# A decoder in one kernel: gated attention's weights and first tiles made in the product keys' last pair

## The reference, cut to what matters

```python
# L0_ffn: product keys
xn = (x - mu) * rsqrt(var + eps) * gamma + beta          # over all tokens
q = (xn @ w_q.T).reshape(b, n, 2, h, kd)                 # h = 8, kd = 128
sim = einsum('pbnhd,hkpd->pbnhk', q, keys)               # 64 keys an axis
s, i = top_k(sim, 8)                                     # then top 8 of the 64 sums
scores, pk = top_k(all_scores, 8); idx = ...             # 64 picks of 4096 rows a token
o = einsum('bnd,bnhkd->bnhk', inputs, key_in[idx])
o = gelu(o) * softmax(scores)
y = einsum('bnhk,bnhkd->bnd', o, key_out[idx])

# L1_attn: gated attention, 16 heads of 16
Q, K, V = (x @ W.T + b for W, b in ((Wq, bq), (Wk, bk), (Wv, bv)))
Qn = Q / max(norm(Q), 1e-12); Kn = K / max(norm(K), 1e-12)      # per head
attn = softmax(Qn @ Kn.T / sqrt(16)); head_outs = attn @ V
h = gelu(x @ Wg1.T + bg1); logits = (h @ Wg2.T + bg2).mean(1)
out = (head_outs * sigmoid(g) * sigmoid(logits)) @ Wo.T + bo
```

## Time and profile before

| | us |
|---|---|
| runs shown | 1965.34, 1972.49, 1965.74; median 1965.74 |
| profiled execution | 1975.05, its span 1973.3 |
| TensorE busy | 1824.4 (92%) |
| VectorE busy | 1331.3 (67%) |
| ScalarE busy | 658.1 (33%) |
| GpSimd busy | 268.0 (14%) |
| mean granted TensorE clock | 0.967 |

### The profile page before, as it was taken

One profiled execution on the slowest core, in us unless ns is written; L12 is line 12 of the kernel. 1 busy time (PEld: TensorE's weight loads), 2 busy tenths in 40 slices (PEclk: granted clock), 3 DMA queues, 4 the chain that ended last, 5 costly groups with the idle time before them and its releaser, 6 DMA issues. The chain is left out here.

```text
span 1973.3 us, 44245 instructions
## 1 busy us (share of the span) xinstructions
PE 1824.4 (92%) x16947; PEld 1539.4 (78%) x16947; DVE 1331.3 (67%) x3614; ACT 658.1 (33%) x1520; POOL 268.0 (14%) x200
## 2 busy tenths in 40 slices
PE   5999999699758999999999959988899999999998
PEld 4888787477557888888888836667788888888887
DVE  4566655377658888989888647746665666666664
ACT  2444443244342212211221126636332323333232
POOL 3222232311010000000000057711000000000000
PEclk9999999799878999999999979989999999999999
DMA  4000000222042000000000040000211111212101
GB/s 161 2 1 0 0 0 1 49 65 64 1 103 38 6 0 5 5 5 0 5 5 0 2 121 1 0 13 27 33 26 23 20 28 16 32 16 32 16 0 43
DMA packets 139266, 47.73 MB, mean 24 GB/s; under 512 B 108178, under 2 KB 138418, under 8 KB 139186
## 3 DMA queue, kind: packets, MB, share of 16 engines
q1 hardware_dynamic: 139186, 46.66, 10.3%
HBM read 42.43 MB, written 4.19 MB: 24 GB/s over the span
## 5 line engine op out<-in xcount | busy, mean ns | idle before, releaser
L2833 ACT ACTIVATE m_silu<-m_gate 128x512 f32<-128x512 f32 x136 | 81.5, 600 | 379.0 <-PE m_gate L621 379.0
L2914 DVE TENSOR_TENSOR m_act_up<-m_silu,m_up 128x512 f32<-128x512 f32 x136 | 93.6, 688 | 168.4 <-PE m_up L621 124.9
L2898 DVE SCALAR_TENSOR_TENSOR g_x<-m_y,m_combine,g_x 128x256 f32<-128x256 f32 x272 | 118.8, 479 | 51.8 <-PE m_y L621 50.3
L237 ACT ACTIVATE a_prob<-a_score,a_neg_max 128x128 f32<-128x128 f32 x256 | 90.7, 367 | 162.5 <-DVE a_neg_max L227 162.5
L2469 PE MATMUL f_out<-f_ko,f_gel 128*128 128x256 f32 x512 | 122.5, 390 | 2.0 <-issue 1.3
L2512 ACT ACTIVATE f_gel<-f_act 128x512 f32<-128x512 f32 x128 | 76.6, 598 | 130.4 <-PE f_act L621 90.9
L2469 PE MATMUL f_turn<-f_ko,f_gel 128*128 128x256 f32 x512 | 111.8, 379 | 0.0
L621 PE MATMUL f_act<-f_hT_pair_high,f_kiT_high 128*128 128x256 f32 x384 | 108.2, 282 | 0.0
L2469 PEld LDWEIGHTS f_out<-f_ko,f_gel 128*128 128x128 f32 x512 | 95.1, 192 | 16.5 <-issue 3.9
L2469 PEld LDWEIGHTS f_turn<-f_ko,f_gel 128*128 128x128 f32 x512 | 97.3, 190 | 13.2
L621 PE MATMUL f_act<-f_hT_pair_high,f_kiT_low 128*128 128x256 f32 x384 | 107.3, 279 | 0.0
(11 more groups left out here) (390 smaller groups left out, 5189.1 us busy)
## 6 DMA issues: line engine op xcount, KB each, us to landing
f_gel<-in_L_ffn_key_in SPq DMA_DIRECT2D x16, 256.0 KB, 4.6
f_ko<-in_L_ffn_key_out SPq DMA_DIRECT2D x2, 2048.0 KB, 19.0
g_shared<-in_ctx SPq DMA_DIRECT2D x8, 256.0 KB, 2.7
fp_wq_nat<-in_L_ffn_w_q SPq DMA_DIRECT2D x8, 256.0 KB, 3.0
h_kept<-fp_hT SPq DMA_DIRECT2D x8, 256.0 KB, 2.6
g_shared<-h_kept SPq DMA_DIRECT2D x8, 256.0 KB, 3.0
g_ctx_next<-in_ctx SPq DMA_DIRECT2D x8, 256.0 KB, 2.7
g_ctx_all<-in_ctx SPq DMA_DIRECT2D x1, 2048.0 KB, 10.6
```

The source lines that it names most:

```text
L237: last = act.activation(self.prob[:, u % 4, j, :], self.score_bank[u % 2][:, j // 2, (j % 2) * P:(j % 2 + 1) * P], ACT.Exp, bias=self.neg_ ...
L2833: act.activation(silu[:, m, :], gate_bank[m][:, :], ACT.Silu).then_inc(silu_ready[m].sem, 1)
L2898: last = dve.scalar_tensor_tensor(x[:, tile, :], y_bank[n][:, t * D:(t + 1) * D], weight, x[:, tile, :], ALU.mult, ALU.add)
L2914: dve.tensor_tensor(act_up[:, m, :], silu[:, m, :], up_bank[m][:, :], ALU.mult) \
```

## The change

Four things.

- The weights, small inputs and first work of gated attention move into the last pair of the product keys, into memory that the low parts (`kiT_low`, `fused_low`) no longer need: SyncE issues the loads when the last activations are done; 7 transpose jobs stand among the outputs of block 0, with all copies on ScalarE; among the outputs of block 1 stand the transposes of pair 0's norm and its two products for queries and keys. VectorE makes the norms of pair 0 and 1 and the statistics of pair 2, empties and sums the squares; GpSimd makes the roots and the two powers of pair 0.
- Gated attention starts with pair 1's norm, and every engine first waits until SyncE has counted up the stage's semaphores (`counts_begun`).
- 28 rows are split in place of 24, so 14 of 16 jobs of the preparation are split ones; the similarities stand behind steps 2 to 5.
- `row_hot` holds three groups in place of four. The last group's rows are made by an instruction of their own behind the first group's weights, into the first group's place. GpSimd's `pair_remainder` waits until the one-hot tiles of the pair before are made.

```diff
 class Turner:
+    def turn(self, pe, n):
+        blocks, _ = self.jobs[n]
+        pe.wait_ge(self.copied[n % 2], n // 2)
+        at = 0
+        for b in blocks:
+            rows = b.shape[0]
+            last = pe.transpose(self.banks[n % 2][:, at:at + rows], b, self.ident[0:rows, 0:rows])
+            at += rows
+        last.then_inc(self.turned[n % 2], 1)
...
+    def all_on_act(self, act):
+        self._copy(act, act.copy, (0, 1))
 # stage_gated_attention
         def _(sp):
-            for n, w in enumerate((w_q, w_k, w_v, w_o)):
-                sp.dma_start(w_nat[:, 2 * n:2 * n + 2, :], w.rearrange("(t p) n -> p t n", p=P)).then_inc(w_loaded, 16)
...
+            sp.sem_inc(counts_begun, 1)
             load_next(sp)
         def _(pool):
-            ln.setup(pool)
-            pool.memset(inv_power[:, :], -0.5).then_inc(power_set, 1)
-            pool.wait_ge(power_set, 1)
-            ln.root(pool, 0)
+            pool.wait_ge(counts_begun, 1)
+            ln.root(pool, 2)
             pool.memset(ones[:, :, :], 0.0).then_inc(masks_cut, 1)
...
-            ln.root(pool, 1)
-            ln.root(pool, 2)
-            for n in range(2):
-                for b in range(2):
-                    invert(n, n, b)
-            pool.wait_ge(loaded, N_LOADS * 16)
+            for b in range(2):
+                given.invert(pool, 1, ss[1], inv[1], b)
         def _(pe):
+            pe.wait_ge(counts_begun, 1)
-            produce(-2, "xn", 0)
-            pe.wait_ge(w_loaded, N_WEIGHTS * 16)
-            turner.on_pe(pe)
-            turner.wait_all(pe)
-            ring.wait_emptied(pe, -2, "xn")
-            produce(-2, "qk0", 0)
-            produce(-2, "qk1", 0)
             produce(-1, "xn", 1)
             produce(-1, "hidden", 0)
         def _(act):
-            empty(-2, "xn", 0, 0)
-            turner.on_act(act)
-            act.wait_ge(loaded, N_LOADS * 16)
-            act.activation(static[:, :], g_row[:, :], ACT.Exp, scale=-1.0).then_inc(static_exp, 1)
-            square(-2, 0, 0, 0)
-            empty(-1, "xn", 1, 1)
-            square(-2, 0, 0, 1)
+            act.wait_ge(given.loaded, given.N_LOADS * 16)
+            empty(-1, "xn", 1, 1)
             act.activation(static[:, :], g_row[:, :], ACT.Exp, scale=-1.0).then_inc(static_exp, 1)
             empty(-1, "hidden", 0, 0)
         def _(dve):
-            ln.statistics(dve, 0)
-            ln.apply(dve, 0)
-            ln.statistics(dve, 1)
-            turner.on_dve(dve)
...
+            dve.tensor_scalar(bg2_neg[:, :], bg2[:, :], -1.0, None, ALU.mult)
+            scale_heads(0, 0, 0)
+            scale_heads(0, 0, 1)
             dve.wait_ge(static_exp, 1)
...
             dve.sem_inc(wide_ready, 1)
-            dve.wait_ge(loaded, N_LOADS * 16)
-            empty(-2, "qk0", 0, 0)
-            ln.apply(dve, 1)
-            empty(-2, "qk1", 0, 0)
-            ln.statistics(dve, 2)
-            sum_squares(0, 0, 0)
-            sum_squares(0, 0, 1)
             empty(-1, "qk0", 1, 1)
             ln.apply(dve, 2)
 # stage_product_keys, preparation
-    SPLIT = 24
+    SPLIT = 28
-                return range(WHOLE + 2 * i, WHOLE + 2 * i + 2) if i < 4 else range(WHOLE + i + 4, WHOLE + i + 5)
+                return range(WHOLE + 2 * i, WHOLE + 2 * i + 2) if i < 6 else range(WHOLE + i + 6, WHOLE + i + 7)
 # stage_product_keys
-        row_hot = s.sb("row_hot", [P, HALF, P], F16)
+        row_hot = s.sb("row_hot", [P, GU - 1, GT, P], F16)
-        TURN_AT, SIMS_AT, SECOND_AT = 0, 3, (23, 24, 26, 28)
+        TURN_AT, SIMS_AT, SECOND_AT = 0, 2, (23, 24, 26, 28)
+        turner = Turner(s, sim_bank, ident, "gated")
+        turner.weight(gated.w_nat, gated.wT, 9)
+        turner.jobs.append(([gated.wg2], gated.wg2T))
+        JOBS_AT = tuple(range(8, 8 + 2 * JOBS, 2))
+        XN_AT, QK_AT = 0, (4, 9)
         def _(sp):
+            sp.wait_ge(act_ready[1], 8 * PAIRS)
+            gated.load(sp)
         def _(pool):
                     pool.wait_ge(h_high, i + 1)
+                    if not (isinstance(i, int) and i == 0):
+                        pool.wait_ge(hot_ready, 2 * i)
...
+            gated.ln.root(pool, 0)
+            gated.ln.root(pool, 1)
+            pool.wait_ge(g_ready[1].sem, g_ready[1].at(NB - 1, 1))
+            pool.memset(gated.inv_power, -0.5).then_inc(gated.power_set, 1)
+            pool.wait_ge(gated.power_set, 1)
+            for b in range(2):
+                gated.invert(pool, 0, gated.ss, gated.inv, b)
         def _(pe):   # weight_group
+                    if m == GU - 1:
+                        pe.wait_ge(last_hot_ready, n + 1)
         # second_weights(r)
+                    if not exists(i + 1) and r in JOBS_AT:
+                        if r == JOBS_AT[0]:
+                            pe.wait_ge(gated.w_loaded, 16 * gated.N_WEIGHTS)
+                            pe.wait_ge(sims_used.sem, sims_used.at(NB, 0))
+                        turner.turn(pe, JOBS_AT.index(r))
+                def gated_queries_and_keys(r):
+                    if exists(i + 1):
+                        return
+                    if r == XN_AT:
+                        turner.wait_all(pe)
+                        gated.ln.transposed(pe, sim_bank[1], ident, 0).then_inc(gated_xn_turned, 1)
+                    if r in QK_AT:
+                        b = QK_AT.index(r)
+                        pe.wait_ge(gated_xn_copied, 1)
+                        token_major(pe, sim_bank[b][:, :], lambda k: gated.xnT[:, k, b * P:(b + 1) * P],
+                                    lambda k: gated.wT[:, k, 0:2 * D]).then_inc(gated_qk_made, 1)
-                outputs(1, lambda r: None)
+                outputs(1, gated_queries_and_keys)
         def _(act):
+            turner.all_on_act(act)
+            act.wait_ge(gated_xn_turned, 1)
+            act.copy(gated.xnT.rearrange("p k t -> p (k t)"), sim_bank[1][:, :]).then_inc(gated_xn_copied, 1)
+            for b in range(2):
+                act.wait_ge(gated_qk_emptied, b + 1)
+                gated.square(act, 0, gated.qk, b)
         def _(dve):
+            def row_hots(at, groups):
+                slot = at % (GU - 1)
+                return dve.tensor_tensor(by_twos(row_hot[:, slot:slot + groups, :, :].rearrange("p m t c -> p (m t) c")),
+                                         per_token(code_twice[:, 0, GT * at:GT * (at + groups), :], P),
+                                         numbers(P, GT * groups), ALU.is_equal)
+            def last_row_hots(i, t):
+                n = 2 * i + t
+                for q in range(2):
+                    dve.wait_ge(g_ready[q].sem, g_ready[q].at(n, 1))
+                row_hots(GU - 1, 1).then_inc(last_hot_ready, 1)
-                dve.tensor_tensor(by_twos(row_hot[:, :, :]), per_token(code_twice[:, 0, :, :], P), numbers(P),
-                                  ALU.is_equal).then_inc(hot_ready, 1)
+                row_hots(0, GU - 1).then_inc(hot_ready, 1)
         # apply_weights
+                    if m == 0:
+                        last_row_hots(i, t)
                     after(m)
         # the loop over pairs
+                if not exists(i + 1):
+                    gated.ln.statistics(dve, 0)
                 one_hot(links, i, 0)
                 choose(links, i, 1)
                 apply_weights(i, 0, lambda m: weigh(links, i, 1) if m == 0 else None)
                 one_hot(links, i, 1)
+                if not exists(i + 1):
+                    gated.ln.apply(dve, 0)
                 apply_weights(i, 1)
                 residual(i, 0)
+                if not exists(i + 1):
+                    gated.ln.statistics(dve, 1)
+                    dve.wait_ge(gated.loaded, 16 * gated.N_LOADS)
+                    empty_queries_and_keys(0)
+                    gated.ln.apply(dve, 1)
+                    gated.sum_squares(dve, 0, gated.ss, 0)
+                    empty_queries_and_keys(1)
+                    gated.ln.statistics(dve, 2)
+                    gated.sum_squares(dve, 0, gated.ss, 1)
```

253 lines of the change are left out of this document (142 added, 111 removed).

## The result

The changed kernel takes 1949.64 us (median of four runs, 1943.33 to 1951.93) against 1968.20 for the kernel before beside it (1965.34 to 1972.49): 0.9899 of it, 95% interval 0.9866 to 0.9931. Run again in two later comparisons it came out at 0.9889 (0.9859 to 0.9918) and 0.9885 (0.9860 to 0.9910). Profile against profile, the span fell from 1973.3 to 1948.7, 24.6; the sum had -22.1.

What follows compares the result with a forecast made beforehand. TensorE was taken to bound the pairs and a chain of waits gated attention's start. Terms -24.0 + 6.5 - 3.6 - 0.7 + 0.4 - 0.7 = -22.1 us took profiled 1975.05 to 1953.0, put at 1943.6 against the median; range 1935 to 1957.

Steps and rivals of the forecast that it cites:

- The start of gated attention, -24.0: From gated attention's beginning to its first scores: work made beforehand shortens the stretch by 24.0 us.
- The 1.6 for GpSimd's clearing beside the scalings: Gated attention's start: GpSimd clearing value tiles holds up VectorE's scalings, 0 to 2.0 us, taken as 1.6.
- The low clock: Gated attention's start: TensorE may begin at 1.2 GHz after the barrier, 0 to 5 us, taken as 0.8.
- The last pair, +6.5 and +0.4: Last product-key pair: moved transposes and products on TensorE's path add 6.5 us; split rows and the one-hot piece add 0.4.
- Six ordinary pairs, -3.6: Ordinary product-key pairs: 0.7 us from split rows less 0.1 makes 0.6 a pair, 3.6 saved over six.
- -1.0 and +1.1: First block's groups, each ordinary pair: moved GpSimd subtraction saves VectorE 1.0 us, the last one-hot piece adds 1.1.
- The preparation, -0.7: Product keys' preparation: fewer transposes ahead, less two more split jobs' ScalarE copies of 0.62 us each, saves 0.7; bounds -1.9 to +1.
- 8 of 16 transposes in 3.76, -1.9: Preparation: two of four copies of unsplit rows no longer stand ahead of the fused keys, saving 1.9 us.
- Late powers: Rival, gated attention's start: one GpSimd power of 5.4 us uncovered and 1.5 more low clock, total -15.2, 1950.5; chance 0.17.
- TensorE alone: Rival, gated attention's start: only TensorE's own 8.5 us of work sets it, -29.5 in place of -24, 1938.1; chance 0.09.
- The piece on the path in every block: Rival, all product-key blocks: the last one-hot piece costs 1.1 us in each of 16, no change, 1959.5; chance 0.07.
- the clock falling in every pair: Rival, all eight pairs: gaps from the new piece drop TensorE's clock, +10.6 us net, 1976, slower; chance 0.05.

Runs made afterwards that it cites:

- x_move_only: Kernel after with 24 rows split, one-hot rows whole, subtraction and similarities as before, so only gated attention's start is moved: 0.9890 of the kernel before.
- x_split24: Kernel after with 24 rows split in place of 28 and padding beside the low parts, all else kept: 0.9881 of the kernel before.
- x_not_moved: Kernel before with 28 split rows, one-hot rows in two pieces, subtraction moved and similarities one step sooner, gated attention not moved: 1.0010 of the kernel before.
- x_bridged: Kernel after with 8 unneeded transposes ahead of the preparation's fused keys and 20 unneeded matmuls in the last pair's waits: 0.9864 of the kernel before.
- x_whole_hot: Kernel before with only the subtraction moved and the similarities one step sooner; one-hot rows whole, 24 rows split: 1.0009 of the kernel before.
- x_early_low: Kernel after without GpSimd's wait for the one-hot rows, so its subtraction falls back beside VectorE's small instructions: 0.9909 of the kernel before.
- x_turned_ahead: Kernel after with the first two groups of split rows turned ahead of the fused keys, 16 transposes before the first products: 0.9876 of the kernel before.
- x_after_again: Kernel after, unchanged, run and profiled again in a later comparison: 0.9889 of the kernel before.
- x_turned_filled: Kernel after with two groups of split rows turned ahead of the fused keys and 20 unneeded matmuls in the last pair: 0.9886 of the kernel before.

## Why the prediction was right, step by step

**The start of gated attention, -24.0: -24.8, right, with two terms wrong against each other.** From the release to the scores 12.65 where the sum had 14.5 (1142.4 to 1156.9). The 1.6 for GpSimd's clearing beside the scalings isn't there: 1.28 for the two, with the clearing begun in their middle. The Trainium skill (SBUF — State Buffer, "Who interferes with whom") had said that a GpSimd instruction that only writes doesn't hold up a VectorE one with two SBUF inputs; by that rule the 1.6 was nothing, and the trace agrees. The low clock was priced at 0.8 and took 1.15 (3.13 against 1.98); the other terms came 0.6 lower together. The release itself came 1.25 later behind the last residual than before (3.50 against 2.2), of which 0.7 was in the sum as SyncE's count.

**The last pair, +6.5 and +0.4: +7.4.** The moved work was sized well: from the start of the outputs to the last residual it is 41.5 in place of 34.2 (1098.79 and 1105.29 to 1140.28 and 1139.52), and 1.1 of the 7.3 is more low clock in the first 16 and 46 output records (2.58 above the 3.69, against 11.69 - 10.17 = 1.52), which leaves 6.2 for the 6.5. x_move_only, without the piece, has 7.1 more than the kernel before. The piece shows in the wait of 2.08, where x_move_only has 1.00 and 0.47.

**Six ordinary pairs, -3.6: -5.8, mis-sized in both halves.** The rows gave 0.50 a pair, not 0.7. "-1.0 and +1.1" for the moved subtraction and the piece failed as a sum of two terms: the first, with the earlier similarities, is -0.2 alone, and the second +0.1 in the room that it opens, because TensorE's own groups are the next bound. Their sum is the -0.1 of the forecast, by another working. With the moved code in place the same three edits are worth more: from x_move_only (67.27) to x_split24 (66.94) it is -0.33, and -0.50 of rows leads on to the kernel after. Another 0.13 to 0.24 comes with the move, though it edits nothing in these pairs: x_move_only has 67.27 against 67.40, and the kernel after 66.44 against 66.68 in x_not_moved. So along this chain the -0.96 is -0.13, -0.33 and -0.50. Why the three edits give more beside the move is not shown.

**The preparation, -0.7: +2.2, wrong.** The step that failed is "8 of 16 transposes in 3.76, -1.9". The transposes did go. But the sum priced every record at the clock of the profile before and took the clock for given; without those 8 TensorE stood at 1.2 GHz for 18.9, where it had been 14.3. Over the runs the preparation of the plain 28-row kernels is 41.7 in the mean of seven (39.58 to 42.48), of the 24-row kernels 37.8 of four (36.88 to 40.18): +3.9. About 1.0 of it is there at an equal clock too (x_bridged, with 8 unneeded transposes in place of those gone, against x_whole_hot), near the 2 x 0.62 that the sum had for the two more split jobs; that leaves 2.9 for the clock. This is what eight pairs at 0.5 bring in, and why the four edits beside the move are worth about nothing. That missing transposes delay the rise is borne out by counts (after 4 to 7 us in six of seven profiles with 16 ahead of the products, in one of seven with 8), not by every profile: x_early_low rose early with 8 and the kernel before late with 16.

**The total is nearer than its terms.** Over the five stretches that the sum priced, the change is -22.0 against -22.1. That is in part luck: the preparation came 2.9 worse and the last pair 0.5, and the ordinary pairs 2.2, the start 0.8 and the first pair 0.2 better. The stretches that it did not price gave another -2.6, of which 2.1 lie ahead of the change.

**From the sum to the microseconds.** Like for like, profile to profile, 1953.0 was forecast and 1950.84 measured. The point of 1943.6 came from taking off the 9.3 by which the profiled run of before lay above the median. That step made the point 6 too low. The runs of before in the later comparisons lie between 1965.05 and 1975.56 with medians of 1970.9 to 1972.8, so the profiled run stood only 2 to 4 above their middle; the three runs at hand had come out low.

**The rivals.** Late powers: no; pair 0's ended 0.5 ahead, pair 1's cost a wait of 0.33. The low clock beside them is real: x_turned_ahead's start is 2.8 longer by it than x_after_again's. TensorE alone: no, it waited 0.41 to 1.10 before each step. The piece on the path in every block, and the clock falling in every pair: no, the pair's granted clock is 1.00 and its wait before the outputs 0.20.

**The signs named in advance.** Scores 12.65 behind the first instruction (14 to 15 forecast), a wait of 0.41 before the queries are turned (under 1), a last pair 7.4 longer (6 to 8), ordinary pairs at 66.4 (66.8), one-hot rows in 3.35 and 1.22 (3.3 and 1.1), small instructions at 0.36 (0.4): all came on the side named, the scores and the ordinary pairs by more than was named. None of them looked at the preparation, where the miss was.

**Open.** Why the clock came up after 14 us in the kernel before and after 5 in x_early_low, with orders of records that gave the opposite elsewhere; what the move does to an ordinary pair; and what x_not_moved lost in the stages behind the pairs (+0.8 and +1.8), which no edit of it touches. None of these was tried further.

## What to carry to other kernels

Work that is taken out of a stretch in which TensorE is at its lower clock may take the clock's rise with it, as it did here in six profiles of seven: price the records behind it at both levels before counting the removal as a gain. When an edit frees the engine that sets the end, ask which engine is next; in the kernels without the move 1.1 us freed on VectorE were worth 0.2, and a piece of 1.2 put back cost 0.1. And judge a change of a few microseconds by the stretches that it touches, from the same instruction to the same instruction, when the scatter of the whole lies in stages ahead of it.

## What the runs showed of the hardware

- The same 32 products behind the same 16 transposes took 6.93 in the kernel before, 4.52 in x_split24 and 3.68 in x_move_only. The records from the start of the preparation on were the same; the moment of the rise was not (14.3, 7.2 and 5.4 behind GpSimd's first instruction).
- A wait of 1.98 was followed by 6.6 us at 0.50 (x_turned_ahead); one of 1.60 in x_turned_filled, and one in x_early_low, by 3.4 us at 0.50 that began some 1.5 behind its end; one of 1.36 in x_bridged, behind eight transposes, by none, nor one of 0.71 in x_move_only. In the last pair waits of 0.72, 2.08 and 0.73 were followed by 16 output records in 6.27 (kernel after) and 5.24 (x_after_again), and waits of 0.72, 1.00, 0.47 and 0.74 by 5.53 (x_move_only); with 35 or 20 unneeded matmuls in them, by 3.69.
- Beside GpSimd's clearing a VectorE instruction on two elements a partition took 0.33, where its like just before the clearing took 0.16; the scaling with two inputs of 512 elements that ran beside it took 0.64 and was not stretched. Beside GpSimd's addition (1164.98, 1.28), which reads SBUF, such a scaling took 1.11 (1165.70); beside one of its powers it took 0.73 (1158.99).
